# Expert rows by transposing DMAs instead of row loads, PE transposes and an ACT copy

## The chip, the cores and the metric

The kernel runs on one core of a Trainium2 chip. The metric is the time of one execution on the device in microseconds, given as the median of several runs. One further execution was recorded by the hardware profiler; all rows below are of that one.

## What is computed

An array x of 8192 tokens (128 graphs of 64 nodes) with 128 features each, and an adjacency matrix of 64 x 64 per graph. Two layers follow one another, each of two parts:

```python
x = x + gnn(layernorm(x), adj, ...)        # masked attention over the 64 nodes of a graph
x = x + ffn(layernorm(x), ...)             # layer 0; in layer 1 the same with other weights
# ffn: 8 experts, the best two of each token:
h = gelu(xe @ W1[e] + b1[e])               # 128 -> 512 (layer 0) or 256 (layer 1)
y = h @ W2[e] + b2[e]                      # back to 128
out = sum over the two experts of weight * y
```

## The kernel before

Each layer has two stages. In the first, `blocks`, eight blocks of 1024 tokens go through attention, the second normalisation and the router. Each token's normalised row is written twice, once for each of its two experts, to `row_buf[L]` in DRAM: POOL issues 128 indirect DMAs per layer (L448) that scatter rows of `ROW_W` = 130 fp32 words = 520 bytes. The first 128 words of a row hold 256 fp16 numbers, the 128 high parts of the features and then the 128 low parts (fp32 split in two fp16 numbers). Words 128 and 129 are tags: the token's number, and which of its experts this is.

The second stage, `groups`, is the one that the change is about. The rows of an expert lie together, and a group is 256 of them (`GRP`, `GT` = 2 tiles of 128). There are `NG` = 71 groups in each layer. Tables in SBUF, made by DVE in `group_tables`, give each group's expert (`grp_ei`) and first row (`grp_ri`). All engines walk the same list of groups:

- SP, `groups` (L365 to L393): after all rows have been scattered it issues the loads of the first four groups (`AHEAD` = 4 buffers), and then `load_next` in order of groups: it waits for the transposes of group g (`gT_ps`, L386) and for `placed` of g (L387), reads the row number of group g+4 from the table (`value_load`, L379), and issues one DMA of 256 rows x 520 bytes to `g_in[k]` (L380).
- PE, `groups` (L591 to L660): `to_feature_rows` waits for the load and transposes the four 128 x 128 fp16 pieces (high and low, two tiles) to PSUM bank 4 or 7 (L602). `up` multiplies by the first weights: 3 matmuls of 256 columns (high x high, low x high, high x low) for each 128 hidden units, so 12 in layer 0 and 6 in layer 1 (L616). `down` multiplies by the second weights: 24 matmuls of 128 columns in layer 0, 12 in layer 1 (L630). The order by hand is: transposes of g+3, up of g+2, down of g.
- ACT, `groups` (L789 to L828): `copy_x` copies the transposed rows from PSUM to `g_xT` (L795, 128 x 512 fp16), and `gelu` is 4 or 2 activations of 128 x 256 (L802), one group behind.
- DVE, `groups` (L1174 to L1233): `place` reads the tags in `g_in` and makes the row numbers of the results (L1182, L1185). `split` rounds the GELU's result to fp16 (L1193) and makes the rest (L1197), 2 instructions of each in layer 0 and 1 of each in layer 1. `finish` waits until the result buffer's last scatter has landed, casts the row numbers (L1207) and adds the bias to PE's result (L1210, `g_y`). The order by hand is: place and split of g+2, finish of g.
- POOL (L452 to L464): after `y_ready` of g it issues two indirect DMAs of 128 rows each to `y_buf[L]` (L456).

PE, ACT and DVE have their lists of groups unrolled eight at a time (`SPAN`), and read the experts of the next eight from the table at the head of a turn. After the last load of layer 0 SP issues the first loads of layer 1 and waits for all results. After the last load of layer 1 it issues the eight loads of the final residual rows (L417) and, when all results have landed, those of the results (L421). After that DVE adds them up.

The order on SP and PE, in its own lines:

```python
                def load_next(g, k):
                    sp.wait_ge(s.gT_ps, g + 1)
                    sp.wait_ge(s.placed, g + 1)
                    load_group(g + AHEAD, k)
...
                        if not last or k + 3 < n:
                            to_feature_rows(k + 3, i)
                        if not last or k + 2 < n:
                            up(g + 2, k % 2, es[k + 2])
                        down(g, k, es[k])
```

Of the kernel before, what the change touches and what calls it, by code (L numbers as in the profile page):

```python
# [5 lines left out]
ALU = mybir.AluOpType  # L6
# [8 lines left out]
P = 128  # L15
# [65 lines left out]
class LayerSems:  # L81
# [3 lines left out]
    def __init__(self, sem, sems, L):  # L85

        self.x_in, self.taken, self.x_done = sems(f"x_in{L}"), sem(f"taken{L}"), sem(f"x_done{L}")
        self.st1, self.st2 = sem(f"st1_{L}"), sem(f"st2_{L}")
        self.xn_ready, self.xT_ps, self.xT_sb = sem(f"xn_ready{L}"), sem(f"xT_ps{L}"), sem(f"xT_sb{L}")
        self.e_ps, self.e_copied, self.e_ready = sem(f"e_ps{L}"), sem(f"e_copied{L}"), sem(f"e_ready{L}")  # L90
        self.hs_ps, self.hs_sb = sem(f"hs_ps{L}"), sem(f"hs_sb{L}")
        self.E_sb, self.ET_ps, self.ET_sb = sem(f"E_sb{L}"), sem(f"ET_ps{L}"), sem(f"ET_sb{L}")
        self.att_ps, self.att_sb = sem(f"att_ps{L}"), sem(f"att_sb{L}")
        self.rinv_ready = sem(f"rinv_ready{L}")
        self.xt_ready, self.xtT_ps, self.xtT_sb = sem(f"xt_ready{L}"), sem(f"xtT_ps{L}"), sem(f"xtT_sb{L}")
        self.lg_done, self.lg_copied, self.hot_ready = sem(f"lg_done{L}"), sem(f"lg_copied{L}"), sem(f"hot_ready{L}")
        self.rexp, self.rank_done = sem(f"rexp{L}"), sem(f"rank_done{L}")
        self.hi_ready = sem(f"hi_ready{L}")
        self.slots_ready, self.x1w_ready = sem(f"slots_ready{L}"), sem(f"x1w_ready{L}")
        self.scattered, self.stored = sems(f"scattered{L}"), sems(f"stored{L}")  # L100

        self.tables, self.pads_out = sem(f"tables{L}"), sem(f"pads_out{L}")
        self.g_loaded, self.y_out = sems(f"g_loaded{L}_", AHEAD), sems(f"y_out{L}_", AHEAD)
        self.gT_ps, self.gT_sb = sem(f"gT_ps{L}"), sem(f"gT_sb{L}")
        self.h_ps, self.act_done, self.h_split = sem(f"h_ps{L}"), sem(f"act_done{L}"), sem(f"h_split{L}")
        self.y_done, self.y_ready, self.placed = sem(f"y_done{L}"), sem(f"y_ready{L}"), sem(f"placed{L}")

# [10 lines left out]
def gnn_moe_kernel(nc, x, adj, gW0, a_src, a_dst, Wr0, br0, ln_g, ln_b, W1_0, b1_0, W2_0, b2_0,  # L118
# [9 lines left out]
    with ExitStack() as ctx:  # L128
# [91 lines left out]
        grp_e, grp_b, grp_c, grp_r = (sb(n, [P, NG]) for n in ("grp_e", "grp_b", "grp_c", "grp_r"))  # L220
        grp_ei, grp_ri = sb("grp_ei", [P, NG], I32), sb("grp_ri", [P, NG], I32)

        g_in = [sb(f"g_in{k}", [P, GT, ROW_W]) for k in range(AHEAD)]
        g_xT = [sb(f"g_xT{q}", [P, 2, GRP], F16) for q in range(2)]

        g_act = [t[:, :, :].rearrange("p t d -> p (t d)").rearrange("p (c r) -> p c r", c=4) for t in (xn, xt)]
        g_h = [t[:, :, :].rearrange("p t d -> p (t d)").bitcast(F16).rearrange("p (h c r) -> p h c r", h=2, c=4)
# [51 lines left out]
        def _(sp):  # L279
# [85 lines left out]
            def groups(L):  # L365
                s = SL[L]
                sp.wait_ge(s.tables, 1)
                for e in range(NE):
                    end = sp.value_load(end_i[0:1, e:e + 1], min_val=0, max_val=NE * CAP - GRP)
                    sp.dma_start(row_buf[L][bass.ds(end, GRP), :].rearrange("(t p) w -> p t w", p=P),  # L370
                                 pad_row[:, :].unsqueeze(1).to_broadcast([P, GT, ROW_W])).then_inc(s.pads_out, 16)
                for q in range(2):
                    sp.wait_ge(s.scattered[q], 16 * TOP * TILES * NBLK // 2)
                sp.wait_ge(s.pads_out, 16 * NE)
                if L == 0:
                    sp.wait_ge(spare_out, 32)

                def load_group(g, k):
                    r = sp.value_load(grp_ri[0:1, bass.ds(g, 1)], min_val=0, max_val=ROWS - GRP)  # L379
                    sp.dma_start(g_in[k][:, :, :], row_buf[L][bass.ds(r, GRP), :].rearrange("(t p) w -> p t w", p=P)  # L380
                                 ).then_inc(s.g_loaded[k], 16)
                for k in range(AHEAD):
                    load_group(k, k)

                def load_next(g, k):
                    sp.wait_ge(s.gT_ps, g + 1)  # L386
                    sp.wait_ge(s.placed, g + 1)  # L387
                    load_group(g + AHEAD, k)
                with sp.Fori(0, NG // AHEAD - 1) as i:
                    for k in range(AHEAD):  # L390
                        load_next(AHEAD * i + k, k)
                for g in range(NG // AHEAD * AHEAD - AHEAD, NG - AHEAD):
                    load_next(g, g % AHEAD)  # L393
# [74 lines left out]
        def _(pe):  # L468
# [121 lines left out]

            def groups(L):  # L591
                s = SL[L]
                x_ps = [bank[b][:, 0:GRP].bitcast(F16).rearrange("p (h n) -> p h n", h=2) for b in (4, 7)]

                def to_feature_rows(k, turn):

                    q, turn = k % 2, SPAN // AHEAD * turn + k // AHEAD
                    pe.wait_ge(s.g_loaded[k % AHEAD], 16 * (turn + 1))
                    rows16 = g_in[k % AHEAD][:, :, :].bitcast(F16)
                    for hl in range(2):  # L600
                        for t in range(GT):
                            last = nc.tensor.transpose(x_ps[q][:, hl, t * P:(t + 1) * P],  # L602
                                                       rows16[:, t, hl * D:(hl + 1) * D], ident16[:, :])
                    last.then_inc(s.gT_ps, 1)

                def experts(g, n):
                    return table_values(mybir.EngineType.PE, grp_ei, g, n, NE - 1)

                def up(g, q, e):
                    wait_past(pe, s.act_done, (g - 1) * NC[L])  # L610
                    pe.wait_ge(s.gT_sb, g + 1)
                    w = w1[L][:, :, :, :].rearrange("p e a h -> p (e a h)")
                    for c in range(NC[L]):
                        dst = bank[2 * q + c // 2][:, (c % 2) * GRP:(c % 2 + 1) * GRP]
                        for m, (wp, xp) in enumerate(((0, 0), (0, 1), (1, 0))):
                            last = nc.tensor.matmul(dst, w[:, bass.ds(e * (2 * HID[L]) + (wp * HID[L] + c * P), P)],  # L616
                                                    g_xT[q][:, xp, :], start=(m == 0), stop=(m == 2))
                        if c % 2:
                            last.then_inc(s.h_ps, 1)

# [15 lines left out]

                pe.wait_ge(s.tables, 1)
                pe.wait_ge(w_ready[L], 1)
                for k in range(2):
                    to_feature_rows(k, 0)  # L640
                es = experts(0, 2)
                up(0, 0, es[0])
                to_feature_rows(2, 0)
                up(1, 1, es[1])

                def turn(i, last=False):

                    n = TAIL if last else SPAN
                    es = experts(SPAN * i, n if last else n + 2)
                    for k in range(n):  # L650
                        g = SPAN * i + k
                        if not last or k + 3 < n:
                            to_feature_rows(k + 3, i)
                        if not last or k + 2 < n:
                            up(g + 2, k % 2, es[k + 2])
                        down(g, k, es[k])
                turn(0)
                with pe.Fori(1, TURNS) as i:
# [17 lines left out]
        def _(act):  # L676
# [111 lines left out]

            def groups(L):  # L789
                s = SL[L]  # L790
                x_ps = [bank[b][:, 0:GRP].bitcast(F16).rearrange("p (h n) -> p h n", h=2) for b in (4, 7)]

                def copy_x(g, q):
                    act.wait_ge(s.gT_ps, g + 1)
                    nc.scalar.activation(g_xT[q][:, :, :], x_ps[q], ACT.Copy).then_inc(s.gT_sb, 1)  # L795

                def gelu(g, q, e):
                    wait_past(act, s.h_split, (g - 1) * (NC[L] // 2))
                    for c in range(NC[L]):
# [8 lines left out]
                load_table(ACT.Gelu)  # L808
                act.wait_ge(s.tables, 1)
                act.wait_ge(w_ready[L], 1)  # L810
                for k in range(2):
                    copy_x(k, k)
                es = experts(0, 2)
                gelu(0, 0, es[0])
                copy_x(2, 0)
                gelu(1, 1, es[1])

                def turn(i, last=False):

                    n = TAIL - 2 if last else SPAN  # L820
                    es = experts(SPAN * i + 2, n)
                    for k in range(n):
                        if not last or k < n - 1:
                            copy_x(SPAN * i + k + 3, (k + 1) % 2)
                        gelu(SPAN * i + k + 2, k % 2, es[k])
                with act.Fori(0, TURNS) as i:
                    turn(i)
# [8 lines left out]
        def _(dve):  # L836
# [337 lines left out]
            def groups(L):  # L1174
# [2 lines left out]

                def place(g, k, turn):

                    dve.wait_ge(s.g_loaded[k], 16 * (turn + 1))  # L1180
                    wait_past(dve, s.placed, g)
                    ch.did(V.tensor_scalar(g_k[:, :], g_in[k][:, :, D + 1], grp_e[:, bass.ds(g, 1)], float(N_TOK),  # L1182
                                           ALU.not_equal, ALU.mult))
                    ch.wait()
                    V.tensor_tensor(g_row[k][:, :], g_k[:, :], g_in[k][:, :, D], ALU.add).then_inc(s.placed, 1)  # L1185

                def split(g, k):

# [94 lines left out]
```

## Time and profile before

| | |
|---|---|
| median of 3 runs | 970.32 us (967.79, 972.44, 970.32) |
| profiled execution, its own time | 966.81 us |
| its span, first to last instruction | 965.0 us |
| granted TensorE clock, mean | 0.823 |
| layer 0 expert stage, first load to all results landed | 236.4 to 464.0 us |
| layer 1 expert stage | 721.4 to about 921 us |
| busy: PE, DVE, ACT, POOL | 69%, 78%, 50%, 57% |

Busy times are of whole engines over the span. The engine names are PE (matmul), PEld (its weight loads, beside the matmuls), DVE, ACT, POOL, and SPq, the queue of SP, whose issuing of DMAs is not counted as busy. In a timeline, a row is a start, a duration, the engine, the line and operation, how many instructions are merged in it, and in brackets how long the engine sat idle before it and what ended that. "issue" means that the profile shows nothing that it waited for.

### The profile page before, as it was taken

To read this page: it belongs to the slowest core of one execution; us is meant where nothing else is said; L and a number is where in the kernel's file an instruction comes from. 1 tells how busy PE (TensorE), PEld (TensorE's weight loads), DVE (VectorE), ACT (ScalarE), POOL (GpSimd) and SP (SyncE) were. 2 spreads that over 40 slices of the span, in tenths; PEclk is the share of its full clock that TensorE was granted. 3 is DMA by queue.
4 is the path that set the end of the run, shared out by engine and by line. 5 is a ranking of instruction groups with operands and counts; after the bars stand their busy time and mean duration, and the time that the engine had idled before them with its cause. 6 is when DMAs were issued, how large, how long until landed. Compare 5 with 4: busy or idle time off the path is not lost.

```text
span 965.0 us, 24021 instructions
## 1 busy us (share of the span) xinstructions
PE 662.5 (69%) x6281; PEld 552.2 (57%) x6282; DVE 753.1 (78%) x2881; ACT 479.1 (50%) x1065; POOL 546.6 (57%) x544
## 2 busy tenths in 40 slices
PE   3977677450999999998078878777208778778400
PEld 2755455350999999998066667666206656556300
DVE  6699999661899999998469989997517777787468
ACT  2466655410777777775146656664206555555200
POOL 0027777765376666767100666666664777777700
PEclk9998989755999999999568777777558998998755
DMA  8283333232233322326524544332333333333899
GB/s 223 81 198 105 104 103 109 75 113 59 67 94 86 86 82 85 87 78 173 142 59 134 140 131 140 89 89 68 93 92 93 99 102 100 97 101 98 224 237 285
DMA packets 168828, 111.51 MB, mean 116 GB/s; under 512 B 30306, under 2 KB 157737, under 8 KB 168776
## 3 DMA queue, kind: packets, MB, share of 16 engines
q1 hardware_dynamic: 151496, 77.04, 30.6%
q0 software_dynamic: 17280, 33.87, 10.6%
q8 instruction: 21, 0.34, 0.2%
q14 instruction: 31, 0.25, 0.1%
HBM read 60.32 MB, written 52.36 MB: 117 GB/s over the span
## 4 chain that ended last, share of the span: by engine, by line
PE 26%; issue 22%; POOL 21%; DVE 21%; DMA 5%; ACT 2%; SPq 1%; POOLq 1%; DVEq 0%; ACTq 0%
POOL row_buf L448 16%; PE bank L616 10%; PE bank L630 9%; POOL y_buf L456 5%; DVE xin L941 4%; DVE stat L886 3%; DVE x1w L993 2%; PE bank L602 2%; DMA y_buf<-g_y,g_dst 2%; PE bank L511 1%; DMA yin<-y_buf 1%; PE bank L528 1%; ACT xn L691 1%; DVE x1w L941 1%; PE bank L515 1%
## 5 line engine op out<-in xcount | busy, mean ns | idle before, releaser
L448 POOL DMA_INDIRECT row_buf<-pay,slot x256 | 255.2, 997 | 235.3 <-DVE slot L1062 155.8
L456 POOL DMA_INDIRECT y_buf<-g_y,g_dst x284 | 291.2, 1025 | 137.2 <-issue 89.9
L616 PE MATMUL bank<-g_xT,w 128*128 128x256 f16 x1278 | 171.4, 282 | 1.5 <-ACT g_xT L795 1.0
L795 ACT ACTIVATE g_xT<-bank 128x512 f16<-128x512 f16 x142 | 84.8, 597 | 170.0 <-PE bank L602 168.1
L616 PEld LDWEIGHTS bank<-g_xT,w 128*128 x1278 | 120.2, 101 | 21.0 <-issue 2.6
L602 PE MATMUL bank<-ident,g_in 128*128 128x128 f16 x568 | 58.3, 228 | 84.4 <-DMA g_in<-row_buf 71.7
L630 PE MATMUL bank<-w,g_h 128*128 x1260 | 86.3, 222 | 18.1 <-DVE g_y L1210 18.1
L802 ACT ACTIVATE xn<-bank,b_cols 128x256 f32<-128x256 f32 x216 | 86.7, 473 | 22.0 <-PE bank L616 15.5
L630 PEld LDWEIGHTS bank<-w,g_h 128*128 128x128 f16 x1260 | 77.8, 99 | 26.9 <-issue 24.7
L802 ACT ACTIVATE xt<-bank,b_cols 128x256 f32<-128x256 f32 x210 | 84.2, 474 | 16.1 <-PE bank L616 12.8
L602 PEld LDWEIGHTS bank<-ident,g_in 128*128 128x128 f16 x568 | 38.2, 102 | 92.4 <-issue 75.7
L1182 DVE TENSOR_SCALAR g_k<-g_in,grp_e 128x2 f32<-128x2 f32 x142 | 33.9, 239 | 47.2 <-DMA g_in<-row_buf 39.1
L691 ACT ACTIVATE xn<-xin,nmr,rstd 128x128 f32<-128x128 f32 x128 | 50.8, 479 | 31.4 <-DVE nmr L930 31.4
L941 DVE SCALAR_TENSOR_TENSOR xin<-yin,xin 128x128 f32<-128x128 f32 x160 | 43.7, 346 | 27.9 <-DMA yin<-y_buf 25.5
L1210 DVE SCALAR_TENSOR_TENSOR g_y<-bank,b_bc 128x256 f32<-128x256 f32 x142 | 59.6, 420 | 0.6 <-PE bank L630 0.6
L492 PE MATMUL bank<-cst,xn 128*128 128x128 f32 x128 | 24.7, 338 | 41.5 <-ACT xn L691 40.2
L528 PE MATMUL bank<-h_sb,pair_eT 128*128 128x137 f32 (+1 forms) x256 | 49.4, 370 | 3.4 <-ACT pair_eT L681 3.4
L511 PEld LDWEIGHTS bank<-to_score,xnT 128*128 128x128 f32 x256 | 41.4, 246 | 17.7 <-issue 17.7
L1207 DVE CAST g_dst<-g_row 128x2 uint32<-128x2 f32 x142 | 25.6, 180 | 31.6 <-DMA y_buf<-g_y,g_dst 31.4
L528 PEld LDWEIGHTS bank<-h_sb,pair_eT 128*128 128x128 f32 x256 | 46.0, 273 | 7.3 <-issue 5.1
L630 PE MATMUL bank<-w,xnT 128*128 x648 | 46.8, 227 | 4.1 <-DVE g_y L1210 4.0
L560 PE MATMUL bank<-cst,tri 128*128 128x512 bf16 x200 | 48.0, 384 | 0.0
(184 smaller groups left out, 1363.0 us busy)
## 6 DMA issues: line engine op xcount, KB each, us to landing
g_in<-row_buf SPq DMA_DIRECT2D x142, 130.0 KB, 2.2
yin<-y_buf SPq DMA_DIRECT2D x24, 512.0 KB, 6.6
x_buf<-x1w SPq DMA_DIRECT2D x16, 520.0 KB, 4.5
xin<-x_buf SPq DMA_DIRECT2D x10, 520.0 KB, 5.6
y_buf<-g_y,g_dst POOLq DMA_INDIRECT x284
xin<-in_x_dram SPq DMA_DIRECT2D x8, 512.0 KB
adj_in<-in_adj_dram SPq DMA_DIRECT2D x16, 256.0 KB
row_buf<-pay,slot POOLq DMA_INDIRECT x256, 2.4
```

The source lines that it names most:

```text
L448: pool.indirect_dma_start(row_buf[L][:, :], bass.IndirectOffsetOnAxis(ap=slot[q][:, k, t:t + 1], axis=0), pay[q][:, t, :], None).then_inc( ...
L456: pool.indirect_dma_start(y_buf[L][:, :], bass.IndirectOffsetOnAxis(ap=g_dst[k][:, t:t + 1], axis=0), g_y[k][:, t, :], None, bounds_check= ...
L511: last = nc.tensor.matmul(bank[2][:, t * NODES:(t + 1) * NODES], xnT[:, t, :], to_score[:, 2 * L, :], start=False, stop=(t % 4 == 3), skip ...
L528: last = nc.tensor.matmul(att_tile[L][t], pair_eT[:, t, :], h_sb[:, t, H_AT:H_AT + att_w[L]], start=True, stop=True)
L602: last = nc.tensor.transpose(x_ps[q][:, hl, t * P:(t + 1) * P], rows16[:, t, hl * D:(hl + 1) * D], ident16[:, :])
L616: last = nc.tensor.matmul(dst, w[:, bass.ds(e * (2 * HID[L]) + (wp * HID[L] + c * P), P)], g_xT[q][:, xp, :], start=(m == 0), stop=(m == 2))
L630: last = nc.tensor.matmul(bank[5 + k % 2][:, t * D:(t + 1) * D], hid[:, hp, c, t * P:(t + 1) * P], w[:, bass.ds(e * (2 * HID[L]) + (2 * c ...
L691: last = nc.scalar.activation(dst[:, t, :], src[:, t, :], ACT.Identity, bias=nmr[:, t:t + 1], scale=rstd[:, t:t + 1])
L795: nc.scalar.activation(g_xT[q][:, :, :], x_ps[q], ACT.Copy).then_inc(s.gT_sb, 1)
L802: nc.scalar.activation(g_act[q][:, c, :], bank[2 * q + c // 2][:, (c % 2) * GRP:(c % 2 + 1) * GRP], ACT.Gelu, bias=b1_cols[L][:, bass.ds(e ...
L941: last = V.scalar_tensor_tensor(src[:, t, X_AT:X_END], y[k][:, t, :], src[:, t, k:k + 1], src[:, t, X_AT:X_END], ALU.mult, ALU.add)
L1210: V.scalar_tensor_tensor(g_y[k][:, :, :], bank[5 + k % 2][:, 0:GT * D].rearrange("p (t d) -> p t d", d=D), 1.0 / (S_H * S_W), flat[:, bass ...
```

## The change

Two transposing DMAs per group, issued by SP, write the high parts and the low parts of the group's 256 rows straight to `g_xT`, feature by feature (128 features on the partitions, 256 rows along them). `g_xT` gets four buffers in place of two. A third DMA brings the two tag words of each row to a new small tile, `g_tag`. `g_in`, the PE transposes, the ACT copy, their semaphores and their use of PSUM banks 4 and 7 go. SP now waits for `h_ps`, the end of `up` of group g, before it loads group g+4. Both layers are changed alike. The diff, cut to its core:

```diff
-        self.gT_ps, self.gT_sb = sem(f"gT_ps{L}"), sem(f"gT_sb{L}")
+        self.g_tagged = sems(f"g_tagged{L}_", AHEAD)
...
-        g_in = [sb(f"g_in{k}", [P, GT, ROW_W]) for k in range(AHEAD)]
-        g_xT = [sb(f"g_xT{q}", [P, 2, GRP], F16) for q in range(2)]
+        g_tag = [sb(f"g_tag{k}", [P, GT, 2]) for k in range(AHEAD)]
+        g_xT = [sb(f"g_xT{k}", [P, 2, GRP], F16) for k in range(AHEAD)]
...
                 def load_group(g, k):
                     r = sp.value_load(grp_ri[0:1, bass.ds(g, 1)], min_val=0, max_val=ROWS - GRP)
-                    sp.dma_start(g_in[k][:, :, :], row_buf[L][bass.ds(r, GRP), :].rearrange("(t p) w -> p t w", p=P)
-                                 ).then_inc(s.g_loaded[k], 16)
+                    rows = row_buf[L][bass.ds(r, GRP), :]
+                    for hl in range(2):
+                        sp.dma_start_transpose(g_xT[k][:, hl, :], rows.bitcast(F16)[:, hl * D:(hl + 1) * D]).then_inc(s.g_loaded[k], 16)
+                    sp.dma_start(g_tag[k][:, :, :], rows[:, D:ROW_W].rearrange("(t p) w -> p t w", p=P)).then_inc(s.g_tagged[k], 16)
...
                 def load_next(g, k):
-                    sp.wait_ge(s.gT_ps, g + 1)
+                    sp.wait_ge(s.h_ps, NC[L] // 2 * (g + 1))
                     sp.wait_ge(s.placed, g + 1)
                     load_group(g + AHEAD, k)
...
-                def to_feature_rows(k, turn):
...
-                def up(g, q, e):
+                def up(g, k, turn, e):
+
+                    q, x = k % 2, k % AHEAD
                     wait_past(pe, s.act_done, (g - 1) * NC[L])
-                    pe.wait_ge(s.gT_sb, g + 1)
+                    pe.wait_ge(s.g_loaded[x], 32 * (SPAN // AHEAD * turn + k // AHEAD + 1))
...
-                                                    g_xT[q][:, xp, :], start=(m == 0), stop=(m == 2))
+                                                    g_xT[x][:, xp, :], start=(m == 0), stop=(m == 2))
...
-                        if not last or k + 3 < n:
-                            to_feature_rows(k + 3, i)
                         if not last or k + 2 < n:
-                            up(g + 2, k % 2, es[k + 2])
+                            up(g + 2, k + 2, i, es[k + 2])
                         down(g, k, es[k])
...
-                def copy_x(g, q):
-                    act.wait_ge(s.gT_ps, g + 1)
-                    nc.scalar.activation(g_xT[q][:, :, :], x_ps[q], ACT.Copy).then_inc(s.gT_sb, 1)
...
                 def place(g, k, turn):
 
-                    dve.wait_ge(s.g_loaded[k], 16 * (turn + 1))
+                    dve.wait_ge(s.g_tagged[k], 16 * (turn + 1))
                     wait_past(dve, s.placed, g)
-                    ch.did(V.tensor_scalar(g_k[:, :], g_in[k][:, :, D + 1], grp_e[:, bass.ds(g, 1)], float(N_TOK),
+                    ch.did(V.tensor_scalar(g_k[:, :], g_tag[k][:, :, 1], grp_e[:, bass.ds(g, 1)], float(N_TOK),
```

## Rows read from the trace of the kernel before

**Rows 1.** Stretches: length, busy us of PE, PEld, DVE, ACT, POOL; granted clock, DMA share.

```profile
236.40:464.00 227.60, 211.02 (x2840) 196.26 (x2840) 201.19 (x568) 154.68 (x357) 149.67 (x142) 0.97 0.32 91
721.40:921.00 199.60, 142.99 (x1562) 113.40 (x1562) 141.19 (x426) 100.44 (x213) 141.56 (x142) 0.88 0.40 111
...
465.00:660.00 195.00, 147.82 (x851) 119.30 (x852) 169.69 (x790) 106.12 (x238) 83.45 (x85) 0.71 0.43 118
...
800.00:860.00 60.00, 46.77 (x512) 36.07 (x509) 47.37 (x140) 33.27 (x71) 45.69 (x47) 0.94 0.35 98
```

**Rows 2.** Timeline of layer 0: one group on DVE, and the GELU before its rounding.

```profile
300.77 1.57 ACT L802 ACTIVATE xn<-bank,b_cols 128x256 f32<-128x256 f32 x4 [0.16 <-DVE g_h L1197]
301.17 0.17 DVE L1207 CAST g_dst<-g_row 128x2 uint32<-128x2 f32 x1
301.24 0.42 DVE L1210 SCALAR_TENSOR_TENSOR g_y<-bank,b_bc 128x256 f32<-128x256 f32 x1
301.57 0.22 DVE L1182 TENSOR_SCALAR g_k<-g_in,grp_e 128x2 f32<-128x2 f32 x1
...
301.93 0.87 DVE L1193 TENSOR_SCALAR xnT<-xn 128x512 f16<-128x512 f32 x2
302.83 1.29 DVE L1197 SCALAR_TENSOR_TENSOR xnT<-xn,xnT 128x512 f16<-128x512 f32 x2
304.04 0.16 DVE L1207 CAST g_dst<-g_row 128x2 uint32<-128x2 f32 x1
```

**Rows 3.** Timeline of layer 0 on PE: one group, and the heads of two turns.

```profile
299.82 1.47 PE L616 MATMUL bank<-g_xT,w 128*128 128x256 f16 x12
...
302.47 0.39 PE L602 MATMUL bank<-ident,g_in 128*128 128x128 f16 x4
302.69 1.47 PE L616 MATMUL bank<-g_xT,w 128*128 128x256 f16 x12
...
293.54 0.39 PE L602 MATMUL bank<-ident,g_in 128*128 128x128 f16 x4 [0.69 <-issue]
...
317.71 0.39 PE L602 MATMUL bank<-ident,g_in 128*128 128x128 f16 x4 [0.71 <-issue]
```

**Rows 4.** Layer 1: a scatter, DVE's wait for one, all of them (first and last start).

```profile
822.30 0.97 POOL L456 DMA_INDIRECT y_buf<-g_y,g_dst  x1 [0.30 <-issue]
...
824.59 0.17 DVE L1207 CAST g_dst<-g_row 128x2 uint32<-128x2 f32 x1 [0.73 <-DMA y_buf<-g_y,g_dst]
...
L456 POOL DMA_INDIRECT y_buf<-g_y,g_dst x142: 967/972/1381, 734.8 to 918.3; - x142
```

**Rows 5.** SP's queue: first loads, a move (ns), waits of 300 to 400 us, landing.

```profile
236.44 3.80 SPq L380 DMA_DIRECT2D g_in<-row_buf  x4
...
L380 SPq MOVE g_in<-row_buf x1: 29/29/29, 305.7 to 305.7; - x1
...
SPq L387 <- DVE g_row L1185: 53.6, 33, 2.4
...
g_in<-row_buf SPq DMA_DIRECT2D x142, 130.0 KB, 2.2
```

**Rows 6.** What is removed: ACT's copies, and the head of layer 0 on PE.

```profile
L795 ACT ACTIVATE g_xT<-bank 128x512 f16<-128x512 f16 x142 | 84.8, 597 | 170.0 <-PE bank L602 168.1
...
238.73 0.58 PE L602 MATMUL bank<-ident,g_in 128*128 128x128 f16 x4 [28.02 <-DMA g_in<-row_buf]
240.70 2.74 PE L616 MATMUL bank<-g_xT,w 128*128 128x256 f16 x12 [0.29 <-issue]
```

**Rows 7.** SP's queue at the ends of the two expert stages.

```profile
464.00 4.08 SPq L291 DMA_DIRECT2D yin<-y_buf  x4
...
895.53 1.80 SPq L417 DMA_DIRECT2D xin<-x_buf  x2
...
904.56 4.39 SPq L417 DMA_DIRECT2D w_stage<-x_buf  x2
920.57 1.84 SPq L421 DMA_DIRECT2D yin<-y_buf  x3
```

More of the change, by code:

```diff
@@ L592, in groups @@
                 s = SL[L]
-                x_ps = [bank[b][:, 0:GRP].bitcast(F16).rearrange("p (h n) -> p h n", h=2) for b in (4, 7)]
-                def to_feature_rows(k, turn):
[L597 to L604, printed above, removed]
                 def experts(g, n):
                     return table_values(mybir.EngineType.PE, grp_ei, g, n, NE - 1)
-                def up(g, q, e):
+                def up(g, k, turn, e):
+                    q, x = k % 2, k % AHEAD
                     wait_past(pe, s.act_done, (g - 1) * NC[L])
-                    pe.wait_ge(s.gT_sb, g + 1)
+                    pe.wait_ge(s.g_loaded[x], 32 * (SPAN // AHEAD * turn + k // AHEAD + 1))
                     w = w1[L][:, :, :, :].rearrange("p e a h -> p (e a h)")
@@ L638, in groups @@
                 pe.wait_ge(w_ready[L], 1)
-                for k in range(2):
-                    to_feature_rows(k, 0)
                 es = experts(0, 2)
-                up(0, 0, es[0])
-                to_feature_rows(2, 0)
-                up(1, 1, es[1])
+                up(0, 0, 0, es[0])
+                up(1, 1, 0, es[1])
                 def turn(i, last=False):
@@ L790, in groups @@
                 s = SL[L]
-                x_ps = [bank[b][:, 0:GRP].bitcast(F16).rearrange("p (h n) -> p h n", h=2) for b in (4, 7)]
-                def copy_x(g, q):
-                    act.wait_ge(s.gT_ps, g + 1)
-                    nc.scalar.activation(g_xT[q][:, :, :], x_ps[q], ACT.Copy).then_inc(s.gT_sb, 1)
                 def gelu(g, q, e):
@@ L810, in groups @@
                 act.wait_ge(w_ready[L], 1)
-                for k in range(2):
-                    copy_x(k, k)
                 es = experts(0, 2)
                 gelu(0, 0, es[0])
-                copy_x(2, 0)
                 gelu(1, 1, es[1])
@@ L822, in turn @@
                     for k in range(n):
-                        if not last or k < n - 1:
-                            copy_x(SPAN * i + k + 3, (k + 1) % 2)
                         gelu(SPAN * i + k + 2, k % 2, es[k])
@@ L1178, in place @@
                 def place(g, k, turn):
-                    dve.wait_ge(s.g_loaded[k], 16 * (turn + 1))
+                    dve.wait_ge(s.g_tagged[k], 16 * (turn + 1))
                     wait_past(dve, s.placed, g)
-                    ch.did(V.tensor_scalar(g_k[:, :], g_in[k][:, :, D + 1], grp_e[:, bass.ds(g, 1)], float(N_TOK),
+                    ch.did(V.tensor_scalar(g_k[:, :], g_tag[k][:, :, 1], grp_e[:, bass.ds(g, 1)], float(N_TOK),
                                            ALU.not_equal, ALU.mult))
                     ch.wait()
-                    V.tensor_tensor(g_row[k][:, :], g_k[:, :], g_in[k][:, :, D], ALU.add).then_inc(s.placed, 1)
+                    V.tensor_tensor(g_row[k][:, :], g_k[:, :], g_tag[k][:, :, 0], ALU.add).then_inc(s.placed, 1)
                 def split(g, k):
```

## The prediction

> **What bounds the kernel now.** I read the page first, then the busy table by stretch, then one group of each expert layer on each engine, then the DMA queue of SP. The page names no single bound: its busy shares (PE 69%, DVE 78%, ACT 50%, POOL 57%, in the table above) are averages over stages. The change touches only the two stretches in which the 71 groups of a layer are worked. The stretches table [rows 1] separates them: 236.4 to 464.0 us is layer 0, 721.4 to 921.0 us layer 1.
>
> Layer 0. A group takes 2.87 us, from one DVE cast to the next (301.17 to 304.04). In it DVE has no gap over 0.04 us [rows 2]: cast and g_y, the tag operations (from 301.57; the second, not shown, fills the time to 301.93), two roundings, two subtractions. PE's turn is as long: four transposes, 12 matmuls up and 24 down, from 299.82 to 302.69 [rows 3]. The two are tied within a hundredth: the fourth GELU ends at 300.77 + 1.57 = 302.34, and the second rounding, which waits for it, starts near 301.93 + 0.44 = 302.37, when DVE is free anyway. So layer 0 has two bounds of equal size, and taking work from one leaves the other. POOL follows g_y; its pair of scatters can be done in 2 x (0.97 + 0.30) = 2.54, as layer 1 shows [rows 4].
>
> Layer 1. Half the hidden width, so PE and DVE have holes. POOL has none: a scatter is 0.97 busy and 0.30 of issue, 1.27 together, and DVE's cast waits 0.73 us for a scatter four groups back to land [rows 4]. From the first scatter at 734.8 to the last at 918.3 are 183.5 us, 2.58 per group [rows 4]. POOL is the bound.
>
> SP, which the change loads, is far from a bound today. Four loads at the start of layer 0, which wait for nothing, span 3.80 us, so (3.80 - 0.37) / 3 = 1.14 us each: 0.37 for the issue and 0.77 for reading the row number and forming the address. Between 300 and 400 us it waited 53.6 us in 33 loads, which leaves (100 - 53.6) / 33 = 1.4 us of its own for a load with the waits' instructions and the loop [rows 5]. I take 1.3 for a turn. SP has 1.5 us free per group in layer 0 and 1.28 in layer 1.
>
> **Removed.** PE: four transposes per group. They take 302.47 to 302.69, 0.22 us of PE's 2.87 in layer 0 [rows 3]. That is 142 x 0.22 = 31 us of PE, but DVE holds layer 0 at 2.87 and POOL holds layer 1 at 2.58. What comes back is little. At the head of a layer, loads land and PE goes 238.69 to 240.70 through two transposes and copies before its first matmul up [rows 6]: 2 us, twice. At every eighth group PE and DVE read the next experts; eight groups take 24.17 us (293.54 to 317.71, with 0.7 of idle PE at each end [rows 3]) against 8 x 2.87 = 22.96, and PE's new slack can take up to 0.8 of the 1.2: at most 7 us in layer 0. ACT: the copy, 597 ns x 142 = 84.8 us [rows 6], and the wait for it. ACT has room (154.7 us busy of 227.6 in layer 0 [rows 1]), so nothing; its cover is that room. Semaphores and PSUM banks 4 and 7: nothing waits for them.
>
> **Moved.** SP waited for the transposes of g and now for h_ps, the end of up(g), later by one up of 1.3 us, and still for placed(g). Load g+4 is needed four groups later, 11.5 us in layer 0 and 10.3 in layer 1, and lands in 2.2 us [rows 5]. Behind that wait stand only SP's later loads. Price nothing; if loads took over 9 us from wait to landing it would show. DVE's tag operations read a small tile in place of g_in, of the same shape (0.22 us for the first [rows 2]): nothing.
>
> **Added.** SP issues three DMAs per group in place of one: two transposing ones of 256 rows x 128 fp16, and the tags, 8 bytes of each row. The tag DMA has the same 256 rows as the present load: 0.37 us of SP, the price that the old load had. Each further DMA brings its own move, 0.029 [rows 5], and register work that I estimate at as much again: with both further ones 0.13 at most, which I take. The transposing issue, c, is in no row. Below: a plain issue of 256 rows, 0.37 us. It cannot be less, since it names the same rows. Above: SP held until the transposed data are in, 2.2 us, issue to landing of a plain one [rows 5]. Between them lies the one row in which an issue has more to work out than equal rows: POOL's DMA_INDIRECT, 0.97 us for 128 rows [rows 4]. The middle of the ends is 1.3; I take c = 1.2, nearer to POOL's row.
>
> The DMA engines move the same bytes in three pieces per row in place of one; their share is 0.32 and 0.40 in the two stretches [rows 1], so this is hidden by the room that they have, unless the pieces cost over twice as much as the row.
>
> So SP's turn becomes 1.3 + 0.13 + 2c = 1.43 + 2c = 3.83 us, over 2.87 and over 2.58. Loads of one queue cannot be overlapped by more buffers: if the issuing takes 3.83 us per group, all engines come to a group per 3.83 us. SP's free 1.5 us hide the first c; the second is bare.
>
> **Sum**, against the profiled execution, 965.0 us of span and 966.81 us as timed. Loads of layer 0 start at 236.4 and end at 236.4 + 71 x 3.83 = 508.3. After the last issue I estimate 13 us: landing 2.5, up 1.3, the rest of GELU 0.8, splitting 2.2, down 1.3, g_y 0.5, POOL's start 0.9 (an estimate), the second scatter 1.3, landing 2.2 [rows 2 to 5]. That is 521.3 against 464.0, where SP goes on to the results [rows 7]: +57.3. Layer 1 starts at 721.4 (its 257.4 us distance unchanged): 721.4 + 271.9 + 11 (half the hidden width) = 1004.3 against 920.6: +83.7. Then the eight final row loads, which SP issues from 895.5 to 904.56 + 4.39 = 909.0 beside the last groups [rows 7], end 2.4 us after the last result has landed: +2.4. In general the extra is 142 p - 400.4 with p the period; 142 x 3.83 - 400.4 = 143.5. 966.8 + 143.5 = 1110 us. The median of the runs, 970.32, stands 3.5 above this execution, inside the runs' own spread of 4.7; I add nothing for it.
>
> **Rivals.**
> Cheap issue (other side, faster), 9%. If c is like a plain issue, SP's turn is 1.43 + 0.74 = 2.17 and stays hidden. The point that decides is c = 0.72 in layer 0 (2.87) and c = 0.58 in layer 1 (2.58). For it: the bytes are the same, and DMA share in these stretches is 0.32 and 0.40 [rows 1]. Then only the heads (-4) and up to -7 at the eighth groups come back: 956 to 963 us. The Trainium skill, "DMA: Bandwidth & Descriptors", in the table of sequencer cycles under Why a DMA increments its semaphore by 16 and not by 1, puts the sequencer's work before that build at 631 cycles for a transposing DMA against 512 for a plain one; scaled on the 0.37 us here that would be c = 0.46, SP's turn 2.35, and about 960 us. The trace shows the plain issue only.
>
> Transposes that block, 6%. SP held until landing, or the queue working one transpose after the other, p = 1.43 + 4.4 = 5.83: 142 x 5.83 - 400.4 = +427, 1394 us. Against it: loads today land in 2.2 us while the next is already issued. The Trainium skill, "VectorE: DVE Perf Modes", The three transpose paths, gives 1309 ns for one 128x128 by DMA; four per group one after the other would be 5.24 us, and 1310 us in all. No row here shows one.
>
> PE's clock falls, 6%, on top of the forecast. With a group every 3.83 us PE works 2.65 in layer 0, 69%. In the blocks at 465 to 660 us it is 76% busy at a granted 0.71; in 800 to 860 78% busy at 0.94 [rows 1]. At the lower level, 1.2 GHz, PE's 2.65 becomes 5.3, above SP's turn: up to (5.3 - 3.83) x 71 = 104 us more, up to 1214. Against it: PE that is short of time is busy throughout, as at 0.97 here. In layer 1 the low level costs 2.6 us per group, hidden.
>
> Middle, c from 0.6 to 0.9, 5%: layer 0 hidden or nearly, layer 1 exposed. c = 0.75 gives p = 2.93, +16: 983; the lower end is no change.
>
> **How the numbers follow.** Forecast, 74%: c from 0.9 to 1.5, p 3.23 to 4.43, 1025 to 1195 us. With the clock case mostly inside, the range 1020 to 1195 holds about 80%. It leaves out the cheap case, the blocking case and the middle. About 0.5%, 4.9 us, is what a measurement of this kernel can tell from no change. Faster: the cheap case less its upper end, 7%. Within 0.5%: that end and a part of the middle, 4%. Slower: the rest, 89%.
>
> **What would show it.** SP issues of L380's successor back to back with no wait on h_ps or placed; the two transposing issues near 1.2 us each and the tag issue 0.37; PE's matmul up waiting for DMA g_xT; DVE 2.87 busy in 3.83; POOL waiting for g_y in layer 1; layer 0 near 285 us and layer 1 near 283 from first load to last landing. If SP still waits for DVE's placed, the issue is cheap and I am wrong on the sign. If SP waits for nothing but issues take over 2 us, or g_xT lands later than 5 us after its issue, the blocking case holds. A granted clock under 0.8 in layer 0 with PE busy throughout is the clock case.

## The result and the profile after

The change makes the kernel slower: 1158.59 us, the median of 4 runs, against 970.50 us before, a ratio of 1.194 (95% interval 1.190 to 1.198). The forecast was 1110 in a range of 1020 to 1195, with a chance of 0.89 for slower. The profiled execution has a span of 1153.6 us against 965.0, 188.6 us more.

Where it went is read in the same stretches as [rows 1]. First the stretches of the changed kernel. Each starts where SP reads the first row number of the layer, 0.7 us before its first load; the first ends where SP goes on to the results, the second 3.9 us before that. The columns are length, then busy us of PE, PEld, DVE, ACT and POOL, granted clock, DMA share and GB/s.

```profile
236.40:548.60 312.20, 211.57 (x2556) 184.06 (x2556) 207.74 (x568) 113.58 (x286) 143.10 (x142) 0.95 0.30 66
804.00:1105.00 301.00, 153.39 (x1278) 118.80 (x1278) 141.31 (x426) 59.62 (x142) 139.56 (x142) 0.72 0.32 70
```

Counted from the first load, as in the table of the kernel before, layer 0's expert stage (237.1 to 548.6) is 311.5 us long and was 227.6; layer 1's runs from 804.6 to the results at 1108.9, 304.3 us, and was 199.2. That is 83.9 + 105.1 = 189.0 us, all of the difference. ACT has 41 us less to do in each, as it should without the copies. No engine is busy for more than 68% of either stretch. The busiest thing is SP's queue, which counts as idle in such a table. Its timeline in layer 1:

```profile
901.34 0.43 SPq L383 DMA_DIRECT2D g_tag<-row_buf  x1
903.02 2.40 SPq L382 DMA_TRANSPOSE g_xT<-row_buf  x2
905.61 0.44 SPq L383 DMA_DIRECT2D g_tag<-row_buf  x1
907.00 2.41 SPq L382 DMA_TRANSPOSE g_xT<-row_buf  x2
909.60 0.44 SPq L383 DMA_DIRECT2D g_tag<-row_buf  x1
911.00 2.40 SPq L382 DMA_TRANSPOSE g_xT<-row_buf  x2
```

Two transposing issues, the tag issue, the read of the next row number, and again, 4.00 us per group. The chain of waits is followed back from the last instruction, at each step to what released it. Before, it ran through PE in layer 0 and POOL in layer 1; now it stays on SP for group after group. One turn of it (start, length, what):

```profile
906.33 0.27 SPq L379
906.63 0.15 SPq L379
906.78 0.05 issue
906.85 0.05 issue
906.90 0.05 SPq L382
906.95 0.04 issue
907.00 1.13 SPq L382
908.13 0.04 issue
908.17 0.04 SPq L382
908.22 0.04 issue
908.26 1.15 SPq L382
909.41 0.04 issue
909.45 0.04 SPq L383
909.49 0.04 issue
909.60 0.44 SPq L383
```

The two transposing issues hold SP for 1.13 and 1.15 us. The rest of the turn of 4.00 us is 1.72: tags 0.44, table read 0.27, register work, and some 0.04 us between any two instructions. Over all 284 of them (ns, least, median, most; then first and last start), and the tag issue under it:

```profile
L382 SPq DMA_TRANSPOSE g_xT<-row_buf x284: 1118/1136/2257, 237.1 to 1090.2; - x142
...
L383 SPq DMA_DIRECT2D g_tag<-row_buf x142: 427/438/1267, 239.7 to 1091.6; - x142
```

The very first of them, at 237.06 with no other before it in the stage, took 1.23 us: the price is not that of a queue which has filled up. What SP does in that time is not shown by any run here.

The waits now (engine and line, what ended them, us in total, times, longest). In [rows 5] SP had waited 53.6 us in a hundred for DVE's `placed`; in the list of SP's own waits there is now no line of the group loads left at all. Instead PE and DVE wait for what SP brings, and ACT and POOL for them. The 286 us of PE include its wait for the first group of each layer, 64 us in both together; 222 are left:

```profile
PE bank L607 <- DMA g_xT<-row_buf: 286.3, 137, 34.7
ACT xn L782 <- PE bank L607: 285.9, 76, 42.8
POOL y_buf L458 <- DVE g_y L1185: 279.6, 130, 20.4
DVE g_k L1157 <- DMA g_tag<-row_buf: 127.0, 94, 22.5
```

### The profile page after: what moved, and what is told of

Its sections match the earlier page's. It is cut to its first block, busy times and chain, and to the rows that moved or that the text cites. A ratio compares the mean times of both kernels' runs of the same rounds, so it can differ in the third digit from the quotient of the medians.

```text
span 1153.6 us, 23157 instructions
## 1 busy us (share of the span) xinstructions
PE 675.3 (59%) x5713; PEld 546.2 (47%) x5714; DVE 759.0 (66%) x2881; ACT 397.1 (34%) x923; POOL 538.6 (47%) x544
## 4 chain that ended last, share of the span: by engine, by line
SPq 43%; DVE 18%; issue 16%; POOL 13%; PE 5%; DMA 3%; ACT 2%; POOLq 0%; DVEq 0%; ACTq 0%
SPq L382 29%; POOL row_buf L450 13%; SPq L383 6%; SPq L379 6%; DVE xin L916 3%; DVE stat L861 2%; DVE x1w L968 2%; PE bank L513 1%; DMA yin<-y_buf 1%; DMA g_xT<-row_buf 1%; ACT xn L677 1%; DVE pay L916 1%; DVE x1w L916 1%; DVE w_stage L916 1%; PE bank L530 1%
## 5 line engine op out<-in xcount | busy, mean ns | idle before, releaser
L458 POOL DMA_INDIRECT y_buf<-g_y,g_dst x284 | 282.7, 995 | 331.8 <-DVE g_y L1185 279.6
L607 PE MATMUL bank<-g_xT,w 128*128 128x256 f16 x1278 | 193.1, 304 | 286.3 <-DMA g_xT<-row_buf 286.3
L1157 DVE TENSOR_SCALAR g_k<-g_tag,grp_e 128x2 f32<-128x2 f32 x142 | 35.0, 246 | 127.8 <-DMA g_tag<-row_buf 127.0
L621 PE MATMUL bank<-w,g_h 128*128 x1260 | 96.7, 238 | 2.2 <-DVE g_y L1185 2.2
L621 PEld LDWEIGHTS bank<-w,g_h 128*128 128x128 f16 x1260 | 89.2, 108 | 6.9 <-issue 2.7
L621 PE MATMUL bank<-w,xnT 128*128 x648 | 50.5, 237 | 0.0
L1168 DVE TENSOR_SCALAR xnT<-xn 128x512 f16<-128x512 f32 x54 | 24.2, 450 | 38.8 <-ACT xn L782 37.9
L621 PE MATMUL bank<-w,xtT 128*128 x648 | 49.6, 237 | 0.0
L1168 DVE TENSOR_SCALAR xtT<-xt 128x512 f16<-128x512 f32 x54 | 24.4, 451 | 36.9 <-ACT xt L782 36.5
L513 PE MATMUL bank<-to_score,xnT 128*128 128x64 f32 x256 | 48.0, 348 | 0.0
```

The costliest lines, as they stand in the source:

```text
L458: pool.indirect_dma_start(y_buf[L][:, :], bass.IndirectOffsetOnAxis(ap=g_dst[k][:, t:t + 1], axis=0), g_y[k][:, t, :], None, bounds_check= ...
L513: last = nc.tensor.matmul(bank[2][:, t * NODES:(t + 1) * NODES], xnT[:, t, :], to_score[:, 2 * L, :], start=False, stop=(t % 4 == 3), skip ...
L621: last = nc.tensor.matmul(bank[5 + k % 2][:, t * D:(t + 1) * D], hid[:, hp, c, t * P:(t + 1) * P], w[:, bass.ds(e * (2 * HID[L]) + (2 * c ...
```

## The experiments

Theory A is that of the prediction: SP's queue sets the period, with a price for each transposing issue. Theory B: the transposition costs time by the byte on the DMA engines. Theory C: the new wait on `h_ps`, or the tags in 8-byte pieces. The kernel before was run again beside these kernels: its median was 970.57 us beside the first four and 971.86 beside the last two, and the ratios are to these.

**One transposing DMA per group.** High and low parts lie side by side in a row, so that one DMA can name both.

```diff
-                    for hl in range(2):
-                        sp.dma_start_transpose(g_xT[k][:, hl, :], rows.bitcast(F16)[:, hl * D:(hl + 1) * D]).then_inc(s.g_loaded[k], 16)
+                    sp.dma_start_transpose(g_xT[k][:, :, :], rows.bitcast(F16)[:, 0:2 * D]).then_inc(s.g_loaded[k], 16)
...
-                    pe.wait_ge(s.g_loaded[x], 32 * (SPAN // AHEAD * turn + k // AHEAD + 1))
+                    pe.wait_ge(s.g_loaded[x], 16 * (SPAN // AHEAD * turn + k // AHEAD + 1))
```

> The changed kernel with one transposing DMA of 256 rows x 256 fp16 per group in place of two of 256 x 128: the same bytes, one issue less. Theory A (SP's issuing sets the period, a price per issue): the second issue of a pair starts 1.27 us after the first in the changed kernel, so the period falls from 4.19 and 4.06 us to 2.92 and 2.79, where layer 0 meets DVE's 2.87 and its turns (3.0 on average): 1158.6 - 71 x 1.19 - 71 x 1.27 = 984, 970 to 1000. Theory B (the transposing itself costs time by the byte on the DMA engines): nothing changes, 1140 to 1165. Theory C (8-byte tag pieces or the new wait on h_ps hold SP): nothing changes either.

Measured: 983.56 us (979.17 to 985.25), 1.0127 of before (1.0087 to 1.0166). Theory A, to within a microsecond of its sum; theory B falls, and so does theory C, since neither the wait nor the tags were changed. The row of the issues in this kernel:

```profile
L381 SPq DMA_TRANSPOSE g_xT<-row_buf x142: 1205/1213/2648, 238.9 to 917.2; - x142
```

Twice the columns cost 1.21 us in place of 1.14. SP still waits for next to nothing in its group loads (once, 0.2 us). In layer 1 its loads are (917.2 - 719.5) / 70 = 2.82 us apart, over POOL's 2.58, and that stage is 18 us longer than before. Layer 0's, with its loads (442.6 - 238.9) / 70 = 2.91 us apart, is 5 us shorter, which leaves the 13 us over before. So one step of the sum was off and the hit is closer than its steps: layer 0 was to meet DVE's turns at 3.0 us per group, but SP sets it too, at 2.91.

**Four transposing DMAs per group**, each of half the rows:

```diff
+                        for t in range(GT):
+                            sp.dma_start_transpose(g_xT[k][:, hl, t * P:(t + 1) * P],
+                                                   rows.bitcast(F16)[t * P:(t + 1) * P, hl * D:(hl + 1) * D]).then_inc(s.g_loaded[k], 16)
```

> The changed kernel with four transposing DMAs of 128 rows x 128 fp16 per group in place of two: the same bytes, two issues more. Theory A: 142 x 2 x 1.27 = 361 us more, about 1519. Theory B: unchanged within 20 us, 1159. If an issue cost by its rows, two half issues would cost as one: 1159 as well.

Measured: 1519.34 us (two runs, 1519.17 and 1519.51), 1.5655 of before. Again theory A's sum, and theory B and a price by rows fall together. One row shows both the price and the landing:

```profile
L383 SPq DMA_TRANSPOSE g_xT<-row_buf x568: 1110/1144/2602, 236.6 to 1453.9; - x190
...
DMA to landing us min/median/max: 2.2/2.3/4.0
```

Half the rows, the same 1.14 us; and such a DMA of 32 KB lands in a median of 2.3 us after its issue, where the plain loads of [rows 5], of 130 KB, took 2.2. The larger ones of the last kernel below, of 128 KB, took 2.7. Transposing makes the data half a microsecond late at most, in the median; it is the queue that it makes late.

**The removed work alone.** The three DMAs are replaced by the one row load of before; nothing is transposed, and `g_xT` holds a constant, so the transposition of the rows is left out.

```diff
-                    for hl in range(2):
-                        sp.dma_start_transpose(g_xT[k][:, hl, :], rows.bitcast(F16)[:, hl * D:(hl + 1) * D]).then_inc(s.g_loaded[k], 16)
-                    sp.dma_start(g_tag[k][:, :, :], rows[:, D:ROW_W].rearrange("(t p) w -> p t w", p=P)).then_inc(s.g_tagged[k], 16)
+                    sp.dma_start(g_in[k][:, :, :], row_buf[L][bass.ds(r, GRP), :].rearrange("(t p) w -> p t w", p=P)
+                                 ).then_inc(s.g_loaded[k], 16)
...
+            for t in g_xT:
+                V.memset(t[:, :, :], 0.5)
```

> The changed kernel with the one row load of the kernel before in place of the three DMAs; PE transposes and the ACT copy stay out, and the matmuls up read a g_xT that is filled once with 0.5 (the transposition of the rows is left out). It shows what the removed work is worth if nothing is added. My steps: PE's 0.22 us per group is tied with DVE in layer 0 and POOL holds layer 1, so 4 to 11 us less than before: 960 to 967. If PE alone bounded layer 0: 71 x 0.22 more, 945 to 952.

Measured: 957.92 us (956.73 to 958.83), 0.987 of before (0.9845 to 0.9895): 12.7 us less than the kernel before, just over my 11. The 31 us of PE work and 85 us of ACT work are worth that much and no more. But the timeline of DVE in layer 0 shows that I had read the tie wrongly. One group of this kernel:

```profile
319.65 0.16 DVE L1183 CAST g_dst<-g_row 128x2 uint32<-128x2 f32 x1
319.72 0.42 DVE L1186 SCALAR_TENSOR_TENSOR g_y<-bank,b_bc 128x256 f32<-128x256 f32 x1
320.05 0.22 DVE L1158 TENSOR_SCALAR g_k<-g_in,grp_e 128x2 f32<-128x2 f32 x1
320.31 0.16 DVE L1161 TENSOR_TENSOR g_row<-g_k,g_in 128x2 f32<-128x2 f32 x1
320.41 0.76 DVE L1169 TENSOR_SCALAR g_h<-xt 128x512 f16<-128x512 f32 x2
321.20 1.29 DVE L1173 SCALAR_TENSOR_TENSOR g_h<-xt,g_h 128x512 f16<-128x512 f32 x2
322.42 0.16 DVE L1183 CAST g_dst<-g_row 128x2 uint32<-128x2 f32 x1
```

The group takes 2.77 us, and the two roundings 0.76; in [rows 2] it was 2.87 and 0.87. A rounding is 0.43 us, and two that don't wait overlap at their ends. So in the kernel before the second rounding did wait for the GELU, by 0.11 us, and the GELU for PE. The chain of waits of the kernel before says the same: between 250 and 460 us PE's matmuls and transposes hold 88% of it and DVE under 1%. PE alone was the bound of layer 0, by a tenth of a microsecond, and behind it came DVE at 2.77. The group at the head of a turn of eight gained more: it took 3.98 us before (318.41 to 322.39 on DVE) and takes 3.07 (316.58 to 319.65). From its first load to the results layer 0's stage is 215.9 us in place of 227.6, and layer 1's 195.4 in place of 199.2. In the profiled execution the first load of layer 0 comes 3.3 us later than before, which no run here explains.

**The added work alone.** The kernel before, complete, with the two transposing DMAs per group into tiles that nothing reads:

```diff
+                    rows = row_buf[L][bass.ds(r, GRP), :]
+                    for hl in range(2):
+                        sp.dma_start_transpose(spare_x[k][:, hl, :], rows.bitcast(F16)[:, hl * D:(hl + 1) * D]).then_inc(s.x_spare[k], 16)
...
                     sp.wait_ge(s.placed, g + 1)
+                    sp.wait_ge(s.x_spare[k], 32 * (turn + 1))
```

> The kernel before, with two transposing DMAs per group beside its row load, into spare tiles that nothing reads; PE transposes, ACT copy and all waits as before. Theory A: SP's turn is that of the changed kernel, about 4.0 to 4.2 us, so 1145 to 1170. Theory C (the wait on h_ps, or the 8-byte tag pieces, cost the time, not the issues): 970 to 1000.

Measured: 1153.51 us (1152.96 and 1154.06), 1.1885 of before (1.184 to 1.193). With the old wait, whole rows and no tag pieces, the time is within 5 us of that of the changed kernel, and the new wait, for the spare tiles, never ended an idle time of SP. Theory C falls here too. Its SP queue in layer 1:

```profile
903.20 0.39 SPq L382 DMA_DIRECT2D g_in<-row_buf  x1
903.72 2.41 SPq L386 DMA_TRANSPOSE spare_x<-row_buf  x2
907.10 0.39 SPq L382 DMA_DIRECT2D g_in<-row_buf  x1
907.62 2.40 SPq L386 DMA_TRANSPOSE spare_x<-row_buf  x2
```

**The same pieces by plain DMAs.** The last kernel with `dma_start` in place of `dma_start_transpose`, to the same spare tiles, token by token:

```diff
-                        sp.dma_start_transpose(spare_x[k][:, hl, :], rows.bitcast(F16)[:, hl * D:(hl + 1) * D]).then_inc(s.x_spare[k], 16)
+                        sp.dma_start(spare_x[k][:, hl, :].rearrange("p (t w) -> p t w", t=GT), rows.bitcast(F16)[
+                            :, hl * D:(hl + 1) * D].rearrange("(t p) w -> p t w", p=P)).then_inc(s.x_spare[k], 16)
```

> The kernel before, with two plain DMAs per group into spare tiles in place of the two transposing ones of the kernel with the added work alone: the same 256-byte pieces of the same rows, the same waits. Theory A (the price is that of the transposing issue, 1.14 us against about 0.4): SP's turn is 1.4 + 2 x 0.55 = 2.5 us, still under 2.87 and just under 2.58: 968 to 985. Rival (any third DMA per group, or the small pieces, costs the time): 1145 to 1170 as with the transposing ones.

Measured: 977.82 us (972.95 to 980.45), 1.0067 of before (1.0041 to 1.0092). Three issues per group are borne almost free if they are plain ones. The 6 us that they cost lie in layer 1, whose loads are now 2.65 us apart and whose stage is 207.2 us in place of 199.2. The pair mostly takes 0.93 us from its first start to its second end, against 2.40:

```profile
853.80 0.37 SPq L382 DMA_DIRECT2D g_in<-row_buf  x1
854.35 0.97 SPq L386 DMA_DIRECT2D spare_x<-row_buf  x2
856.41 0.38 SPq L382 DMA_DIRECT2D g_in<-row_buf  x1
857.01 0.93 SPq L386 DMA_DIRECT2D spare_x<-row_buf  x2
```

**One DMA, and one read of the table for four groups.** This takes the rest off SP's turn:

```diff
-                    r = sp.value_load(grp_ri[0:1, bass.ds(g, 1)], min_val=0, max_val=ROWS - GRP)
...
+                first_rows = lambda g, n: table_values(mybir.EngineType.SP, grp_ri, g, n, ROWS - GRP)
...
                 with sp.Fori(0, NG // AHEAD - 1) as i:
-                    for k in range(AHEAD):
-                        load_next(AHEAD * i + k, k)
+                    for k, r in enumerate(first_rows(AHEAD * i + AHEAD, AHEAD)):
+                        load_next(AHEAD * i + k, k, r)
```

> One transposing DMA per group, and SP reads the row numbers of four groups from the table at once, at the head of its loop, in place of one for each group. Theory A (SP's turn is the sum of what its queue issues and reads): the one-DMA kernel's turn of 2.8 us loses three of four table reads of about 0.7 us with their register work, so about 2.2 to 2.3, under POOL's 2.58 in layer 1 and under DVE in layer 0. Then all that the removed work is worth comes back: 957.9 of the kernel with the saving alone, and 1 to 2 us more at each head, where a transposing DMA lands later: 958 to 964, under before by 6 to 12 us. If the latency or the flow of the transposing DMAs, not SP's issuing, holds the one-DMA kernel at 983.6, it stays there: 978 to 985.

Measured: 956.86 us (952.04 to 958.23), 0.985 of before (0.9816 to 0.9884). It beats the kernel before and the changed one. It equals the kernel with the saving alone, though it does the whole computation with real transposes. SP waits for DVE again, as it did before the change, so its issuing is hidden:

```profile
SPq L388 <- DVE g_row L1160: 39.3, 56, 1.8
```

Where it neither waits nor reads the table its turn is 2.05 us (from 863.16 to 865.21). The turn with the read of four numbers takes 2.66 (from 718.62 to 721.28), so the mean of four is about 2.2, under DVE's 2.77 and POOL's 2.58:

```profile
863.16 1.23 SPq L380 DMA_TRANSPOSE g_xT<-row_buf  x1
864.59 0.41 SPq L381 DMA_DIRECT2D g_tag<-row_buf  x1
865.21 1.20 SPq L380 DMA_TRANSPOSE g_xT<-row_buf  x1
```

## Why the prediction was right, and where it was not

The mechanism was right: SP's queue is the one place where the change adds more than it removes, the loads cannot be issued faster than it works, and every engine comes to one group per turn of SP. The one-DMA and four-DMA kernels, at 984 and 1519 us, hit the sums that were made with this mechanism and the measured 1.27 us from one issue of a pair to the next. The time itself was forecast from one term that was guessed and one that was too small, as follows.

- Price of the transposing issue: taken as 1.2, from an end at 0.37 and one at 2.2 and POOL's scatter between. Measured 1.14. That the guess was this near, and with it the sign, is in part luck: POOL's scatter is another operation on another engine, and nothing in the trace of before excluded 0.37, with which the change would by my sum have been a gain. The kernel with plain pieces shows how little two issues at that price cost: 6 us with nothing removed.
- The rest of SP's turn: taken as 1.43, measured 1.72 in an ordinary turn of layer 1, and more where the loop closes every fourth group (from 901.34 to 903.02, 1.68 us against 1.39). This is the term that was mis-sized. The tag issue took 0.44 in place of 0.37, and I had put the register work and the 0.04 us between two instructions of the queue at less than they are. The mean distance of the loads was (532.7 - 239.7) / 70 = 4.19 us in layer 0 and (1091.6 - 807.3) / 70 = 4.06 in layer 1, against 3.83. The difference, 71 x 0.36 + 71 x 0.23, is 42 us. The forecast was made against the profiled execution, which took 1155.4 us after the change, so it was 45 us short there; the ends below add 7, and small differences at the starts take off 4. The median, 1158.6, stands 3 us higher.
- The ends of the stages: 13 and 11 us after the last issue; measured 548.6 - 532.7 = 15.9 and 1108.9 - 1091.6 = 17.3. The +2.4 for the final row loads did not arise as such: SP was through with them at 1106.0 and then still waited for results.
- The removed work: worth 4 to 11 us if nothing were added; 12.7 measured. The heads gave the 2 us each that were forecast (from the first load to the first matmul up 4.3 and 4.1 us before, 2.3 and 2.3 with the saving alone), and the group at the head of a turn came 0.8 us nearer to an ordinary one, the most that was forecast (from 3.98 - 2.87 = 1.11 us over it to 3.07 - 2.77 = 0.30). What failed is that DVE holds layer 0 at 2.87: "two bounds of equal size", "tied within a hundredth", was wrong. The instruction after the GELU started when DVE would have been free by my reckoning, because I had spaced two roundings at 0.44; unheld they come 0.33 apart. A start that fitted a wait to 0.03 us should have been checked as one.
- The moved wait: priced at nothing, rightly. It never ended an idle time of SP.
- Cheap issue: fell with 1.14 us. The sequencer cycles, 631 for a transposing DMA of small tiles against 512 for a plain one, that the Trainium skill gives in "DMA: Bandwidth & Descriptors", Why a DMA increments its semaphore by 16 and not by 1, would give an estimate of 0.46. The trace does not agree: 1.14 to 0.37 is a factor of three.
- Blocking: fell. The queue is free again after 1.14 us, while the data take 2.3 us or more to land. The 1309 ns for one 128x128 of the Trainium skill, "VectorE: DVE Perf Modes", The three transpose paths, isn't a price per block in a stream: the one-DMA kernel with one read moves four such blocks in a turn of 2.05 us.
- PE's clock: it fell in layer 1, from 0.88 to a granted 0.72, with PE busy about half of the time, and stayed at 0.95 in layer 0. Neither cost anything that shows: after its first groups PE still waited 222 us for `g_xT`.

What is not settled: why a transposing issue takes 1.14 us. Three of the 284 took over 2 us (at 280.2, 292.6 and 878.8), some 3 us in all, and no run shows what held them. Nor does a run show what they would cost on ACT's queue.

## What to carry to other kernels

Count the turn of the queue that issues, in instructions and by their own rows, as one counts an engine: it does not appear in the busy shares, and a queue with 1.3 to 1.5 us free per group has room for two more plain DMAs (0.93 us) but not for two transposing ones (2.40 us). A transposing DMA from DRAM costs SP by the issue, not by the byte, in the sizes tried here (1.14 us for 128 or 256 rows of 128 fp16, 1.21 us for 256 rows of 256), so give it as many columns as one destination can take, and read table values for several of them at once. Then moving transposes from PE to the DMA is a gain, though only of what the next bound leaves: 15 us here for 116 us of removed work.

## What the runs showed of the hardware that I had not expected

Halving a transposing DMA did not make its issue shorter (1.144 us for 128 rows, 1.136 for 256), and doubling its columns added only 0.08. It landed nearly as soon as a plain load: 2.3 us for 32 KB and 2.7 for 128 KB, against 2.2 for a plain 130 KB. And two DVE instructions of 0.43 us, neither of which waits, start 0.33 apart, so that a pair's length, 0.76 or 0.87, tells whether the second one waited.
